# Two streams of a transformer-and-scan kernel: the next sequence's front moved into the FFN, scan units recut, mask on TensorE, one-hots and a quarter of the products on GpSimd

## The chip, the cores and the metric

The kernel runs on one core of a Trainium2 chip. The metric is the device time of one launch in microseconds (us), lower is better. It computes two post-norm decoder layers for 16 sequences of 256 tokens with 256 features.

## The reference

Each line is followed by a residual add and a layer norm (`x = layernorm(x + f(x))`):

```
layer 0  mamba:   xin, z = split(x @ W_in)            # 512 channels each
                  xc = silu(causal_conv4(xin) + conv_b)
                  dt, Bm, Cm = split(xc @ W_xproj)    # 64, 16, 16 columns
                  dt = softplus(dt @ W_dt + b_dt)
                  h_t = exp(dt_t * A) * h_{t-1} + dt_t * B_t * xc_t   # 512 x 16 states, 256 steps
                  y_t = sum_n(h_t * C_t);  out = ((y + xc * Dp) * silu(z)) @ W_out
         latent cross-attention: 16 heads of 16; each query attends to 64 keys given by
                  itok (with repeats: a count of each key acts as weight, no count as mask)
         FFN with quantised activations and ternary weights, 256 -> 1024 -> 256, gelu, layer norm inside
layer 1  self-attention (16 heads of 16), cross-attention (16 heads of 64),
         mixture of 8 experts (top 6) and a shared expert
```

## The kernel before

**Two streams.** Layer 0 of sequence i (the x stream: `mamba`, `latent`, `ffn`, `ffn_end`) runs at the same time as layer 1 of sequence i-1 (the y stream: self-attention, cross-attention, experts). Every engine has one instruction list. Each engine's part of either stream is written as a generator whose `yield`s cut it into steps, and `ORDER` says by hand for each engine in which turn steps of x and y are taken ("x9 y3 ..."). Nothing reorders it later: an instruction that waits holds up all that stands behind it on its engine. The engines meet in semaphores. PSUM (`ps`) has eight banks pairs-wise called `bank(n)`: 0 to 3 for x, 4 to 7 for y. `region_x` and `region_y` are SBUF scratch that the stages of a stream reuse.

**The mamba stage.** TensorE (PE) projects x with `win` in four parts (L497, `projected`). ScalarE (ACT) scales by the last tap (L983), VectorE (DVE) adds the other three taps (L1383, twelve operations of 128x256), ACT takes silu. PE multiplies by `wxd` (low rank, L516), `wc` and `wb` (C and B with each of the 16 rows repeated over 8 partitions, L519, L549) and `wdt` (L543), and ACT and DVE compute softplus (L1406 to L1411) and dt times xc (L1413). The rows of dt and dt·xc go to DRAM (`rows_of_dt`) and come back spread over partitions, 64 DMAs a sequence of 256 KB each (L329, `spread_rows`, four slots each).

**The scan** is cut into 32 units. A unit has 8 channels x 16 states on the partitions and two channel groups along the free axis: ACT forms the decay by two exponentials into PSUM (L1028), DVE the product dtx·B (L1432, `product`, B read from PSUM), then the scan (L1449), POOL (GpSimd) multiplies by C (L1227), and PE sums the states (L561).

**Counts and masks.** The 64 indices of each query are split in two digits (`digits`). DVE writes one-hot rows of both digits (L1351, `one_hots`), PE multiplies them query by query (L471, `counted`, four parts of 32), turns the result (L480, `counts_turned`) and turns it again by key (L489); DVE makes `cntq`, `mask` and `cntk` of it (L1361, L1362, L1368). In `narrow_attention` of the latent stage, DVE takes the row maximum of the scores under the mask with a custom operation for each half (L1482, 32 a sequence, each with a read of its accumulator and half of them with a memset); self-attention has no mask and takes one plain reduce for four (L1486).

**The FFN of x** is w1 (L694), gelu, norm, quantisation, turns (L706), w2 (L713). The one-hots and counts of the next sequence are already taken in it; the projection, convolution and all that follows come behind it.

## Time and profile before

| | us |
|---|---|
| median of 3 runs | 3937.22 (3931.72 to 3943.57) |
| the profiled execution | 3951.12, of it span 3949.3 |
| PE busy | 3210.4 (81%) |
| DVE busy | 3004.6 (76%) |
| ACT busy | 1953.3 (49%) |
| POOL busy | 650.5 (16%) |
| steady period of one sequence | 232.8 |

The span is the time from the first to the last instruction in the trace. The period was read in the middle of the run, and is cut in three stages: A from the end sum of the latent stage to the first product of the scan (FFN and front of x, experts of y), B to the last scan, C (latent attention of x, rest of cross-attention of y) to the next sum.

### The profile page before, as it was taken

The page shows a single profiled execution, that of the slowest core. Times are in us where ns is not written, and L with a number is a line of the kernel's source. Part 1 is how long each engine was busy: PE and PEld are TensorE (multiplying, and loading weights), DVE is VectorE, ACT ScalarE, POOL GpSimd, SP SyncE. Part 2 cuts the span into 40 slices and gives each one's busy share as a digit, 9 for nine tenths or more (in the row PEclk, how much of TensorE's full clock was granted, in tenths as well). Part 3 has the DMA queues.
Part 4 walks back from the last instruction along what each step waited for, and adds up shares of the span by engine and source line. Part 5 has one row for each costly group of instructions (what it writes and reads, how often), then busy time and mean ns, then how long its engine had stood idle before and what let it go on. Part 6 is the DMA issues. An engine that isn't in the chain of part 4 may idle for free.

```text
span 3949.3 us, 57618 instructions
## 1 busy us (share of the span) xinstructions
PE 3210.4 (81%) x21250; PEld 2199.1 (56%) x21250; DVE 3004.6 (76%) x6496; ACT 1953.3 (49%) x4513; POOL 650.5 (16%) x516
## 2 busy tenths in 40 slices
PE   2468988788797888978888897988879888887877
PEld 1245656556464655646556564655646565564655
DVE  5678796877878688796868879687887868778632
ACT  2336455564545546455554645555464554645422
POOL 0303030120303012040210304021030301204000
PEclk8679999999999989999999999989999998999987
DMA  6526171532716235181523517153361614427100
GB/s 213 131 56 174 50 197 63 157 119 89 203 50 184 77 123 153 54 238 49 155 95 116 171 50 225 52 159 99 96 196 50 197 63 146 130 74 215 55 31 16
DMA packets 205833, 470.84 MB, mean 119 GB/s; under 512 B 23856, under 2 KB 43952, under 8 KB 190832
## 3 DMA queue, kind: packets, MB, share of 16 engines
q1 hardware_dynamic: 205552, 467.17, 39.2%
q8 instruction: 167, 2.74, 0.3%
q14 instruction: 114, 0.93, 0.1%
HBM read 446.11 MB, written 20.97 MB: 118 GB/s over the span
## 4 chain that ended last, share of the span: by engine, by line
PE 41%; DVE 34%; ACT 9%; issue 8%; DMA 6%; SPq 1%; POOL 0%; DVEq 0%; ACTq 0%
DVE region_x L1449 7%; PE ps L864 6%; DMA region_x<-rows_of_dt 5%; DVE region_x L1432 5%; PE ps L633 4%; PE ps L824 3%; PE ps L810 3%; PE ps L497 3%; ACT region_y L1148 3%; PE ps L845 3%; PE ps L614 2%; DVE nm L1486 2%; PE ps L645 2%; DVE x_stats L1284 2%; PE ps L569 2%
## 5 line engine op out<-in xcount | busy, mean ns | idle before, releaser
L1227 POOL TENSOR_TENSOR region_x<-region_x 128x512 f32<-128x512 f32 x512 | 650.3, 1270 | 2982.6 <-DVE region_x L1449 2982.6
L1028 ACT ACTIVATE ps<-region_x,aneg 128x255 f32<-128x255 f32 x1024 | 443.1, 470 | 446.2 <-DVE region_x L1449 431.3
L1449 DVE TENSOR_TENSOR_SCAN region_x<-ps,region_x 128x512 f32<-128x512 f32 x512 | 622.9, 1217 | 16.0 <-ACT ps L1028 15.1
L1432 DVE TENSOR_TENSOR region_x<-region_x,ps 128x512 f32<-128x512 f32 x512 | 343.1, 671 | 49.2 <-DMA region_x<-rows_of_dt 46.2
L864 PE MATMUL ps<-xTy,wide 128*128 128x256 f32 x1280 | 307.1, 395 | 0.0
L1148 ACT ACTIVATE region_y<-ps,rmax 128x256 f32<-128x256 f32 x512 | 235.7, 500 | 140.9 <-DVE rmax L1591 140.9
L1499 DVE SCALAR_TENSOR_TENSOR region_x<-region_x,cntk 128x512 f32<-128x512 f32 x256 | 167.0, 689 | 156.2 <-ACT region_x L1066 156.2
L864 PEld LDWEIGHTS ps<-xTy,wide 128*128 128x128 f32 x1280 | 244.5, 196 | 42.3 <-issue 10.1
L561 PE MATMUL ps<-region_x,sely 128*32 128x512 f32 x1024 | 157.5, 691 | 121.6 <-POOL region_x L1227 121.3
L614 PE MATMUL ps<-region_y 64*128 64x256 f32 x1024 | 176.9, 485 | 91.5 <-DVE VP L1572 37.4
L633 PE MATMUL ps<-region_y 64*128 64x256 f32 x1024 | 173.1, 464 | 95.9 <-ACT region_y L1066 49.5
L1591 DVE TENSOR_REDUCE rmax<-ps 128x4 f32<-128x1024 f32 x128 | 153.2, 1218 | 111.2 <-PE ps L791 109.7
L1482 DVE CUSTOM_DVE_ANT_0 region_x<-ps,mask 128x256 f32<-128x256 f32 x512 | 184.7, 420 | 40.1 <-issue 40.1
L925 PE MATMUL ps<-down,region_y 128*128 128x256 f32 x640 | 183.4, 454 | 37.2 <-DVE region_y L1650 37.2
L1164 ACT ACTIVATE region_y<-ps 128x512 f32<-128x512 f32 x256 | 140.6, 597 | 142.1 <-PE ps L813 142.1
L633 PEld LDWEIGHTS ps<-region_y 64*128 64x128 f32 x1024 | 103.0, 217 | 190.9 <-ACT region_y L1066 131.3
L614 PEld LDWEIGHTS ps<-region_y 64*128 64x128 f32 x1024 | 113.4, 236 | 155.0 <-DVE nm L1486 60.6
L1066 ACT ACTIVATE region_x<-ps 128x512 f32<-128x512 f32 x256 | 141.2, 605 | 86.6 <-PE ps L633 86.6
L925 PEld LDWEIGHTS ps<-down,region_y 128*128 128x128 f32 x640 | 146.0, 233 | 64.9 <-issue 38.7
L791 PE MATMUL ps<-region_y 64*128 64x256 f32 x1024 | 138.7, 406 | 41.7 <-DVE region_y L1586 24.6
L1066 ACT ACTIVATE region_y<-ps 128x512 f32<-128x512 f32 x256 | 138.3, 593 | 52.9 <-PE ps L633 52.0
L810 PE MATMUL ps<-region_y 64*128 64x256 f32 x1024 | 156.5, 397 | 8.9 <-ACT shiftT L1157 7.6
(246 smaller groups left out, 6491.9 us busy)
## 6 DMA issues: line engine op xcount, KB each, us to landing
region_x<-rows_of_dt SPq DMA_DIRECT2D x1024, 256.0 KB, 5.3
wide<-in_wgate SPq DMA_DIRECT2D x16, 1280.0 KB, 8.4
wide<-in_wup SPq DMA_DIRECT2D x16, 1280.0 KB, 11.0
down<-in_wmoe SPq DMA_DIRECT2D x16, 1280.0 KB, 5.6
wide<-in_wq SPq DMA_DIRECT2D x16, 1024.0 KB, 4.8
wide<-in_wk SPq DMA_DIRECT2D x16, 1024.0 KB, 6.9
wide<-in_wv SPq DMA_DIRECT2D x16, 1024.0 KB, 8.9
down<-in_wo SPq DMA_DIRECT2D x16, 1024.0 KB, 7.8
```

Source lines behind the costliest of these rows:

```text
L614: last = mm(ps[:, b + j, qt * T:(qt + 1) * T], a.QT[r, t, qt * P:(qt + 1) * P], a.KT[u % 2][r, t, :], start=True, stop=True)
L633: last = mm(ps[:, a.sT_bank(n + j), kt * T:(kt + 1) * T], a.KT[e][r, t, kt * P:(kt + 1) * P], a.QT[r, t, :], start=True, stop=True)
L810: mm(ps[:, b, kt * T:(kt + 1) * T], KT2[r, t, kt * P:(kt + 1) * P], QT2[r, t, :], start=True, stop=False)
L864: last = mm(bank(b)[:, j, :], w[:, k, f * P:(f + 1) * P], xTy[:, k, :], start=(k == 0), stop=(k == KD - 1))
L925: last = mm(bank(7)[:, tt, :], mhT[:, f, tt * P:(tt + 1) * P], wmoe[:, f, :], start=(n == 0), stop=(n == KM - 1))
L1028: last = f(ps[:, 1 + 2 * (k % 2), m * T + 1:(m + 1) * T], dt_rep[k % SLOTS][:, m, 1:T], ACT.Exp, scale=aneg[:, k, m:m + 1])
L1066: f(a.PT[:, n % 8].rearrange("p k q -> p (k q)"), ps[:, a.sT_bank(n), :], ACT.Exp).then_inc(a.probs, 1)
L1148: last = f(junk2[:, 4 * (u % 2) + 2 * qt + g], ps[:, a.pair_bank(u) + g, qt * T:(qt + 1) * T], ACT.Exp, bias=rmax[:, qt, g, u:u + 1], accu ...
L1227: nc.gpsimd.tensor_tensor(hbuf[k % HSLOTS], hbuf[k % HSLOTS], csb.unsqueeze(1).to_broadcast([P, 2, T]), ALU.mult).then_inc(hc_ready, 1)
L1432: tt_(hbuf[k % HSLOTS], dtx_rep[k % SLOTS], ps[:, 2, 0:T].unsqueeze(1).to_broadcast([P, 2, T]), ALU.mult).then_inc(dbx, 1)
L1449: nc.vector.tensor_tensor_scan(flat(hbuf[k % HSLOTS]), ps[:, 1 + 2 * (k % 2), :], flat(hbuf[k % HSLOTS]), 0.0, ALU.mult, ALU.add).then_inc ...
L1482: last = nc.vector.tensor_tensor_reduce(a.junk[:, 4 * (u % 2) + 2 * qt + j], ps[:, b + j, qt * T:(qt + 1) * T], mask[:, qt, :], -1.0, HUGE ...
```

## The change

1. **Front inside the FFN.** `projected`, the convolution, silu, `low_rank`, dt, the first half of softplus and all one-hots of sequence i+1 are issued inside `ffn(i)`; `counted`, `c_and_b` and `counts_turned` at its end. The digits move to the latent stage. `region_x` grows, so that the buffers live beside those of the FFN.
2. **Convolution.** ACT forms all four tap products from PSUM (16 operations a sequence), POOL adds them (6 of 128x512). DVE's twelve operations go.
3. **Low rank, B and C.** One matrix `wx` of 96 columns (4 matmuls) and four matmuls with `rep`, which repeats the rows, stand for the twelve of `wxd`, `wc` and `wb`. ACT copies C and B to SBUF.
4. **Scan units.** A unit has 16 channels x 8 states on the partitions and two halves of the states along the free axis. Both halves use the same dt row, so a spread DMA brings 128 KB in place of 256 KB, and there are eight slots. The sum over states now has 64 matmuls of 256 columns in place of 32 of 512.
5. **Mask on PE.** `mask` is bf16, and two matmuls with the identity bring it into PSUM ahead of the scores (16 a sequence, 128x512). The maximum is the plain reduce (now L1573).
6. **One-hots on POOL** (L1310, 48 of 128x128), and every fourth product too (L1333). Also from DVE to ACT: the adds of `bdt` (4), the copy to `VP0`, the scaling of `QT2` (4).
7. New order tables for all engines (one row shown).

```diff
-SLOTS = 4
+SLOTS = 8
...
-    "pe": (67, "x9 y3 x1 y13 x1 y2 x1 y6 x1 y4 x1 y7 x1 y4 x1 y3 x1 y5 x1 y1 x1 y1 x2 y2 x1 y2 x5 y3 x1 y1 x1 y1 x1 "
+    "pe": (60, "y2 x1 y12 x1 y7 x1 y5 x1 y3 x1 y8 x1 y3 x1 y7 x2 y1 x1 y1 x2 y2 x1 y2 x5 y2 x2 y1 x1 y1 x1 y2 x1 y2 "
...
-                pair, s, j = k // 16, k % 16 // 4, k % 4
-                first = 32 * j + 8 * s
-                rows = scratch[i % 2, what][first:first + 8, 512 * pair:512 * pair + 512]
-                return sp.dma_start(dst.rearrange("p m t -> p (m t)"), rows.unsqueeze(0).to_broadcast([NS, 8, 512]))
+                m, e, j = k // 8, k // 4 % 2, k % 4
+                first = 32 * j + 16 * e
+                rows = scratch[i % 2, what][first:first + 16, T * m:T * m + T]
+                return sp.dma_start(dst, rows.unsqueeze(1).to_broadcast([16, 8, T]))
...
+                    if a.masked:
+                        pe.wait_ge(cnt_max, i + 1)
+                        for j in range(2):
+                            mm(ps[:, b + j, :], W["identb"][:], mask[:].rearrange("p q k -> p (q k)"), start=True, stop=False)
...
+                if more:
                     pe.wait_ge(f_h, at(i, TT, 2))
-                    yield from counted(i + 1, 0, 2)
+                    projected(i + 1, 2)
+                    projected(i + 1, 3)
+                    yield from low_rank(i + 1)
+                    pe.wait_ge(silu_z, i + 2)
+                    yield from counted(i + 1, 0, 1)
...
+            def conv_products(i, half):
+                act.wait_ge(xz, at(i, 4, half + 1))
+                act.wait_ge(digit_step, at(i, DIGIT_STEPS, DIGIT_STEPS))
+                if half:
+                    act.wait_ge(conv_sum, at(i, 6, 3))
+                for j in range(2):
+                    m = 2 * half + j
+                    f(conv[:, m, :], bank(half)[:, j, :], ACT.Identity, bias=W["convb"][:, m:m + 1],
+                      scale=W["convw"][:, m, TAPS - 1:TAPS])
+                    for k in range(TAPS - 1):
+                        late = TAPS - 1 - k
+                        last = f(taps[k][:, j, late:T], bank(half)[:, j, 0:T - late], ACT.Copy,
+                                 scale=W["convw"][:, m, k:k + 1])
+                last.then_inc(taps_sb, 1)
...
+            def one_hot(o, digit, first, last):
+                for value in range(first, last):
+                    ins = nc.gpsimd.tensor_scalar(o[:, :, value], digit, float(value), None, ALU.is_equal)
+                return ins
+
+            def next_sequence(i):
+                pool.wait_ge(digit_step, at(i, DIGIT_STEPS, DIGIT_STEPS))
+                if i:
+                    pool.wait_ge(X.sum_ps, at(i - 1, 3, 2))
+                one_hot(oh_lo, lob, 0, 16)
+                conv_sums(i, 0)
+                one_hot(oh_hi, hib, 0, 8)
+                conv_sums(i, 1)
+                one_hot(oh_hi, hib, 8, 32).then_inc(onehot, 1)
...
+                for k in range(UNITS):
+                    if k % 4 == 2 and k + 5 < UNITS:
+                        product(k + 5)
                     pool.wait_ge(h_ready, at(i, UNITS, k + 1))
...
-                    if a.masked:
-                        if u >= 2:
-                            v.wait_ge(a.rmax, at(i, 8, u - 1))
-                        for qt in range(TT):
-                            nc.vector.memset(spare[:, 6 + 2 * (u % 2) + qt:7 + 2 * (u % 2) + qt], 0.0)
-                            for j in range(2):
-                                col = 64 * j + 32 * (u % 2) + 16 + t
-                                last = nc.vector.tensor_tensor_reduce(
-                                    a.junk[:, 4 * (u % 2) + 2 * qt + j], ps[:, b + j, qt * T:(qt + 1) * T], mask[:, qt, :],
-                                    -1.0, HUGE, ALU.add, ALU.min, a.NM[:, qt, col:col + 1])
```

**TensorE, from the last counts of the FFN to the turn of the counts, before.** L471 are the counts (`counted`), L925 the experts' down projection of y, L706 and L713 the turns and w2 of the FFN, L497 the projection, L516 to L549 low rank, C, dt and B, L480 the counts turned.

```order
L471 MATMUL ps<-region_x 32x16 x32
L925 MATMUL ps<-down,region_y 128x256 x10
L706 MATMUL ps<-identb,region_x 128x128 x16
L713 MATMUL ps<-w2q,region_x 128x256 x16
L471 MATMUL ps<-region_x 32x16 x32
L497 MATMUL ps<-xTx,win 128x256 x4
L471 MATMUL ps<-region_x 32x16 x32
L497 MATMUL ps<-xTx,win 128x256 x12
L516 MATMUL ps<-region_x,wxd 64x256 x2
L519 MATMUL ps<-region_x,wc 128x256 x2
...
L543 MATMUL ps<-region_x,wdt 128x256 x4
...
L480 MATMUL ps<-identb,region_x 128x32 x16
```

The same stretch of TensorE after, in two pieces: first from the cross-attention's output (L864, L845 before) on, then the end. L502 is the projection, L883 the experts (L864 before), L889 the routing weights, L511 `wx`, L518 `wdt`, L478 the counts, L529 and L534 `rep`, L487 the counts turned.

```order
L864 MATMUL ps<-down,region_y 128x256 x16
L502 MATMUL ps<-xTx,win 128x256 x8
L466 MATMUL ps<-ident,xh 128x128 x4
L873 MATMUL ps<-router,xTy 128x8 x4
L883 MATMUL ps<-xTy,wide 128x256 x8
L687 MATMUL ps<-identb,region_x 128x128 x2
...
L883 MATMUL ps<-xTy,wide 128x256 x4
L502 MATMUL ps<-xTx,win 128x256 x8
L883 MATMUL ps<-xTy,wide 128x256 x4
L889 MATMUL ps<-wT,selx 128x256 x2
L883 MATMUL ps<-xTy,wide 128x256 x8
L511 MATMUL ps<-region_x,wx 96x256 x4
```

```order
L518 MATMUL ps<-region_x,wdt 128x256 x2
L478 MATMUL ps<-region_x 32x16 x32
L717 MATMUL ps<-identb,region_x 128x128 x8
L944 MATMUL ps<-down,region_y 128x256 x10
...
L478 MATMUL ps<-region_x 32x16 x32
L730 MATMUL ps<-w2q,region_x 128x256 x16
L529 MATMUL ps<-region_x,rep 128x256 x2
L534 MATMUL ps<-region_x,rep 128x256 x2
L944 MATMUL ps<-down,region_y 128x256 x10
L478 MATMUL ps<-region_x 32x16 x64
L487 MATMUL ps<-identb,region_x 128x32 x16
```

The projections and low rank have moved from behind w2 to between the experts' matmuls, and only the B and C rows, half of the counts and their turn still stand behind w2. All 16 matmuls of the cross-attention's output (L864) stand behind the latent output now; before, they stood ahead of it in two halves, with the latent stage's turns between them (L662, L668).

**VectorE, from the end of the FFN to the first scan, before.** L1395 adds `bdt`, L1361 to L1362 are `cntq` and `mask`, L1406 to L1413 softplus and dt·xc, once for each half.

```order
L1395 TENSOR_SCALAR region_x<-ps,bdt 128x256 x2
L1361 COPY cntq<-ps 128x256
L1362 TENSOR_SCALAR mask<-ps 128x256
L1361 COPY cntq<-ps 128x256
L1362 TENSOR_SCALAR mask<-ps 128x256
L1406 TENSOR_SCALAR region_x<-region_x 128x512
...
L1368 COPY cntk<-ps 128x512
L1406 TENSOR_SCALAR region_x<-region_x 128x512
...
L1416 MEMSET ps 128x2 x2
L1432 TENSOR_TENSOR region_x<-region_x,ps 128x512 x2
```

VectorE there after; L1495 is dt·xc of the second half, L1475, L1476 and L1482 are `cntq`, `mask` and `cntk`, L1529 the product and L1549 the scan.

```order
L1495 TENSOR_TENSOR region_x<-region_x 128x512
L1505 MEMSET ps 128x2
L1475 COPY cntq<-ps 128x256
L1476 TENSOR_SCALAR mask<-ps 128x256
L1475 COPY cntq<-ps 128x256
L1476 TENSOR_SCALAR mask<-ps 128x256
L1482 COPY cntk<-ps 128x512
L1511 MEMSET ps 128x2
L1529 TENSOR_TENSOR region_x<-region_x,ps 128x512 x2
L1549 SCALAR_TENSOR_TENSOR region_x<-ps,region_x 128x512
```

Softplus and dt·xc of both halves now stand ahead of the masks instead of behind them.

**GpSimd after**, from the last units of one sequence on (before, its whole list is the multiplications by C): L1341 are these, L1310 the one-hots, L1306 the sums of the convolution, L1333 the products.

```order
L1341 TENSOR_TENSOR region_x<-region_x 128x512 x6
L1310 TENSOR_SCALAR region_x<-region_x 128x128 x16
L1306 TENSOR_TENSOR region_x<-region_x 128x512 x3
L1310 TENSOR_SCALAR region_x<-region_x 128x128 x8
L1306 TENSOR_TENSOR region_x<-region_x 128x512 x3
L1310 TENSOR_SCALAR region_x<-region_x 128x128 x24
L1333 TENSOR_TENSOR region_x<-region_x 128x512
L1341 TENSOR_TENSOR region_x<-region_x 128x512 x2
```

Ahead of TensorE's first count (L478) all 48 one-hots have to be done.

## Rows read from the trace of the kernel before

**Rows 1.** The page: busy time, and the chain that ended last, by engine.

```profile
PE 3210.4 (81%) x21250; PEld 2199.1 (56%) x21250; DVE 3004.6 (76%) x6496; ACT 1953.3 (49%) x4513; POOL 650.5 (16%) x516
...
PE 41%; DVE 34%; ACT 9%; issue 8%; DMA 6%; SPq 1%; POOL 0%; DVEq 0%; ACTq 0%
```

**Rows 2.** Windows: us, busy PE, PEld, DVE, ACT, POOL; clock, DMA share, GB/s.

```profile
1606.60:1684.60 78.00, 67.65 (x442) 52.94 (x442) 67.64 (x166) 36.64 (x63) 0.00 (x0) 0.96 0.21 76
1684.60:1765.00 80.40, 60.91 (x366) 35.67 (x368) 76.15 (x102) 42.15 (x97) 39.44 (x32) 0.92 0.83 231
1765.00:1839.40 74.40, 68.06 (x524) 46.85 (x520) 42.65 (x140) 43.07 (x123) 1.23 (x1) 1.00 0.15 58
sum 232.80, PE 196.62 PEld 135.47 DVE 186.45 ACT 121.85 POOL 40.67; mean PE 65.54 PEld 45.16 DVE 62.15 ACT 40.62 POOL 13.56
```

**Rows 3.** The chain in stage A, its last part: start, us, link.

```profile
1653.17 1.05 PE ps L713 x8
...
1669.39 1.92 PE ps L549 x8
1671.32 1.11 PE ps L480 x16
...
1688.67 1.13 DVE region_x L1449
```

**Rows 4.** TensorE's timeline near the end of stage C (two records a matmul).

```profile
1828.22 3.72 PE L845 MATMUL ps<-down,region_y 128*128 128x256 f32 x16
...
1832.65 3.62 PE L845 MATMUL ps<-down,region_y 128*128 128x256 f32 x16
```

**Rows 5.** Groups by line and form: busy us, mean ns, idle before them.

```profile
L1227 POOL TENSOR_TENSOR region_x<-region_x 128x512 f32<-128x512 f32 x512 | 650.3, 1270 | 2982.6 <-DVE region_x L1449 2982.6
L1432 DVE TENSOR_TENSOR region_x<-region_x,ps 128x512 f32<-128x512 f32 x512 | 343.1, 671 | 49.2 <-DMA region_x<-rows_of_dt 46.2 <-DMA rows_of_dt<-region_x 1.0
L1482 DVE CUSTOM_DVE_ANT_0 region_x<-ps,mask 128x256 f32<-128x256 f32 x512 | 184.7, 420 | 40.1 <-issue 40.1
L1482 DVE DVE_READ_ACCUMULATOR2_ANT nm<- 128x1 f32 x512 | 42.7, 83 | 0.0
L1486 DVE TENSOR_REDUCE nm<-ps 128x4 f32<-128x1024 f32 x128 | 153.0, 1216 | 12.8 <-PE ps L614 9.4
L1383 DVE SCALAR_TENSOR_TENSOR region_x<-region_x,convw 128x256 f32<-128x256 f32 x192 | 84.6, 482 | 22.2 <-ACT region_x L983 19.3
L1351 DVE TENSOR_TENSOR region_x<-region_x,iota 128x1024 bf16<-128x1024 bf16 x64 | 77.6, 1212 | 0.1
L1351 DVE TENSOR_TENSOR region_x<-region_x,iota 128x512 bf16<-128x512 bf16 x64 | 43.8, 685 | 0.0
L1586 DVE TENSOR_SCALAR region_y<-ps 128x512 f32<-128x512 f32 x64 | 42.3, 681 | 15.9 <-PE ps L779 15.9
L983 ACT ACTIVATE region_x<-ps,convb,convw 128x256 f32<-128x256 f32 x64 | 32.4, 562 | 0.0
L694 PE MATMUL ps<-w1q,region_x 128*128 128x512 bf16 x128 | 31.9, 395 | 0.7 <-ACT region_x L1084 0.7
```

**Rows 6.** VectorE's timeline in stage B.

```profile
1706.59 1.22 DVE L1449 TENSOR_TENSOR_SCAN region_x<-ps,region_x 128x512 f32<-128x512 f32 x1
1707.72 0.66 DVE L1432 TENSOR_TENSOR region_x<-region_x,ps 128x512 f32<-128x512 f32 x1
1708.31 1.22 DVE L1449 TENSOR_TENSOR_SCAN region_x<-ps,region_x 128x512 f32<-128x512 f32 x1
...
1720.15 0.69 DVE L1432 TENSOR_TENSOR region_x<-region_x,ps 128x512 f32<-128x512 f32 x1 [1.15 <-DMA region_x<-rows_of_dt]
```

**Rows 7.** Timeline at 1743.7, and line L1297's instructions (ns lowest, median, highest).

```profile
1743.69 1.26 POOL L1227 TENSOR_TENSOR region_x<-region_x 128x512 f32<-128x512 f32 x1 [0.44 <-DVE region_x L1449]
1743.70 1.28 DVE L1297 SCALAR_TENSOR_TENSOR y_nt<-y_nt,y_rstd 128x2 f32<-128x2 f32 x1
...
L1297 DVE SCALAR_TENSOR_TENSOR y_nt<-y_nt,y_rstd x48: 160/161/1280, 342.0 to 3945.6; 128x2 f32<-128x2 f32 x48
```

## Prediction before the change was run

> **What bounds the kernel now.** I read the page first [rows 1]. TensorE is busy for 81% of the span and VectorE for 76%, and the chain that ended last is split between them, 41% and 34%; neither alone is the bound, so I cut one steady period in the three stages named above and read the windows [rows 2]. In A TensorE works 67.65 of 78.0 us and VectorE 67.64. In B VectorE works 76.15 of 80.4 us and TensorE 60.9. In C TensorE works 68.1 of 74.4 and VectorE 42.7. So VectorE sets B, TensorE sets C, and A has both near 87%. For A I read the chain [rows 3]: TensorE is on it without a break from w2 at 1653.2 to the end of the turned counts at 1672.4, then come masks, softplus and the DMA round trip of the dt rows, and the first scan starts at 1688.7. From TensorE's last turn to the first scan pass 16.2 us, in which TensorE has other work but VectorE has no scan.
>
> The profiled execution took 3951.12 us, 1.82 more than its span; the median of the runs is 0.9965 of it. All sums below are made against the span.
>
> **VectorE's removals, per sequence.** From the groups [rows 5], each divided by 16 sequences. The taps: 84.6 / 16 = 5.3 us. The one-hots: (77.6 + 43.8) / 16 = 7.6. The masked maximum: (184.7 + 42.7) / 16 = 14.2 and 16 memsets, under 1 us together, replaced by eight plain reduces of 1.216 as self-attention has, 9.7: 5 saved. Eight products: 8 x 0.67 = 5.4. Four `QT2` scalings: 42.3 / 16 = 2.6, the `VP0` copy at the same price 0.7, and four adds of `bdt` of half that width, 0.4 each, 1.7. In all 28 of 186.5 us, so VectorE needs about 158.
>
> **TensorE.** It gains 16 bf16 matmuls of 512 columns with the mask. The group of w1, the same form, has 31.9 / 128 = 0.25 us each: +4.0. Four matmuls fewer in the projection of B, C and low rank, at 1.92 / 4 = 0.48 [rows 3]: -2. The sum over states keeps its columns; its extra 32 issues lie in B, where TensorE has 19 us idle, and cost nothing there (at 0.1 us each they would be 3). So TensorE goes from 196.6 to about 199, and it becomes the engine that all hangs on: below 199 no period can go, and 232.8 - 199 is what packing could give at most.
>
> **ACT and POOL.** ACT takes 12 more tap products at 0.5 (the group of the last tap has 0.56 on average [rows 5]), the `bdt` adds, copies and `QT2`, and gives up some: 121.9 to about 133. POOL goes from 40.7 to: 38 + 8 of 1.27 more for products, 6 x 1.27 = 7.6 for sums, and 48 one-hots. A one-hot of one input and 128 columns is not in the trace. POOL's two-input operation costs 1.27 / 512 = 2.5 ns a column, so 128 columns are 0.32, and with something fixed I take 0.39. Bounds: 0.15 (VectorE's per-column price, 1.212 / 1024, on 128 columns), and 1.27 for a whole one of the widest form seen. At 0.39 it is 18.7 us a sequence, and POOL has 78 us of 233.
>
> *The skill on this.* The Trainium skill, "GPSIMD Engine Reference", § Engine selection, has two-input elementwise work about twice as slow on GpSimd as on VectorE and one-input work at about line rate; the product row agrees (1.27 against 0.67), and by line rate a one-hot would be nearer my lower bound than the upper.
>
> **Stage A after.** TensorE's list in A: before, 65.8 us lay between the latent sum and the end of L480 (1672.4 - 1606.6). Now the 16 matmuls of the cross-attention's output (3.7 + 3.6 = 7.3 [rows 4]) lie behind the latent output, and 2 go: 71.1 if every idle stays. The windows show 10.3 us of TensorE idle in A; without any it would be 61. I followed the new list by hand against ACT (tap products to 13.6 us after the sum, second half 17.5 to 21.5, since `conv_products` waits for POOL's first sums; w1's start at 24.6, against 23.4 before) and against POOL (last one-hot at 34.7, first count due at 46.7, so 12 us of slack), and get the turned counts' end at 67.0. Behind it VectorE no longer waits for softplus and the dt rows: these are done during the FFN, and the spread DMAs are under way. There remain the turn by key (behind eight query projections, 3.9 us), one copy, a memset and the product: first product at 72.5 at the earliest. I add 1.5 for hand-overs that the walk leaves out, and 3 for the shared lock.
>
> The lock is in the trace: a VectorE operation of 128x2 whose median is 0.16 us takes 1.28 beside a POOL operation of 1.26, and ends with it [rows 7]. POOL was idle in A [rows 2]; now it works some 26 us there (18.7 + 7.6), while VectorE has about 40 operations with two SBUF inputs. One in three meets POOL (26 of 78), and loses half of 0.39 or of 1.27: near 3 us. From below it is 0, if VectorE waits for others anyway; from above half of POOL's time, 13. So A comes to 77, against 78.0.
>
> **Stage B after.** VectorE's work 76.2, less eight products at the spacing with which they stand between scans (1708.31 - 1707.72 = 0.59 [rows 6]), 4.7, less `QT2`'s 2.4, plus the self-attention's scaling that now falls in it (1.9): 71. The idle was 4.3 us, of which 46.2 / 16 = 2.9 waiting for the spread DMAs, as in the row at 1720.15. The DMA share in B is 0.83. Halving the bytes at the same count of packets gives something between no relief (a packet costs its turn) and half; with eight slots I take 2.5 of idle. B = 73.5. POOL does not bind: per unit it needs 1.27 x 1.25 = 1.59, VectorE 1.13 + 0.75 x 0.59 = 1.57 of scan and product (1707.72 - 1706.59 = 1.13) plus its y work.
>
> **Stage C after.** TensorE sets it: 74.4 - 7.3 (moved to A) + 4.0 (mask) - 0.6 (its waits for the masked maximum) = 70.5.
>
> **Sum.** 77 + 73.5 + 70.5 = 221.0 against 232.8: 11.8 a period, 15 periods, 177. The first sequence has no FFN to hide in: its one-hots cost 18.7 on POOL in place of 7.6, the sums 2.3 more and the taps wait for them, some +15, less 7 for the shorter way to the first scan: +8. Span 3949.3 - 177 + 8 = 3780; with 1.82 and 0.9965: **3769 us**.
>
> **Rivals.**
> *R1, slower: the one-hots hold up TensorE.* The first count waits for all 48, and behind it stand turns, w2 and the experts' down projection. By the walk the slack is 12 us over 48 operations: it decides at 0.39 + 12 / 48 = 0.64 that a stall begins, and it eats the gain of 11.8 at 0.9. At 1.27 the stall is 48 x 1.27 - 30.7 = 30: period 251, span near 4270. At 1.1 the period is 243 and the time 4130 (15 x 22 us, and as much once in the first sequence). For it speaks that POOL's fixed cost is nowhere to be read beside a strided write, against it that the two-input operation itself is 2.5 ns a column. 0.06, at some 4130.
> *R2: A does not get denser.* The lock, the wait of the second tap products for POOL, and ACT's longer list push w1 and all behind it: 6 us more, A = 83, period 227, 3860. For it: 40 operations against a busy POOL, and ACT's 0.5 us steps stand before qT and gelu. 0.15. The Trainium skill, "SBUF — State Buffer", § Who interferes with whom, says that a VectorE operation with two SBUF inputs and a GpSimd one that reads SBUF block each other wholly; the row at 1743.7 agrees (1.28 for 0.16), and the page speaks against handing POOL work in A.
> *R3: the new order packs TensorE.* If its share in B also rises as VectorE's 28 us fall away, and A and C lose idle, 199 / 0.94 = 212, span 3641, 3634. For it: VectorE falls to 158 and nobody else is above 133. Against: each of TensorE's idles in A is a dependence inside a stream. 0.14.
> *R4: no change*, the FFN's stage growing by all that the scan's saves: 0.03.
>
> **Chances.** The forecast has 0.62, own range 3720 to 3815 (the lock 0 or 6, the DMA idle 0 or 3, hand-overs, times 15). The range for all, 3660 to 3865, takes in R2 and the slower half of R3. About 0.3% is what a measurement can tell here. Faster: 0.62 + 0.15 + 0.14 = 0.91; same 0.03; slower 0.06.
>
> **What would show it.** The period near 221, TensorE's busy share near 0.9 from 0.81; L1310 near 0.39 us, ended before the first L478 wants it; first product 73 to 80 us behind the latent sum; no DMA behind the first scan; VectorE at 158 a period; L1529's wait for spread DMAs under 1 us a sequence. Wrong would be: TensorE waiting for POOL's L1310 or for ACT's tap products at w1, or two-input VectorE operations in A near 1.3 us.

## The result, and the profile after

The changed kernel takes 4131.91 us (median, 4130.08 to 4133.3) against 3940.39 of the kernel before in the same series: 1.0484 of its time, 95% interval 1.0462 to 1.0506. The forecast was 3769. The time that came is that of the rival R1, which had 0.06.

The page of the changed kernel: busy time, the chain that ended last by engine, and by line.

```profile
PE 3258.6 (79%) x22402; PEld 2261.6 (55%) x22402; DVE 2714.0 (66%) x4787; ACT 2040.2 (49%) x4788; POOL 1744.8 (42%) x1508
...
PE 40%; POOL 20%; DVE 13%; ACT 12%; issue 6%; DVEq 0%; ACTq 0%; POOLq 0%
POOL region_x L1310 18%; PE ps L608 6%; DVE region_x L1549 5%; PE ps L944 4%; PE ps L627 4%; PE ps L749 4%; ACT ps L1066 3%; PE ps L843 3%; PE ps L829 3%; DVE region_x L1529 3%; POOL region_x L1306 3%; PE ps L810 2%; PE ps L639 2%; ACT region_y L1215 2%; PE ps L604 2%
```

VectorE's busy time has fallen from 3004.6 to 2714.0 us, which is 18 us a sequence where 28 were forecast, and the waits for spread DMAs are gone from the chain [rows 1]. But GpSimd, which had 0% of it, now holds a fifth of it, nearly all with the one-hots (L1310). The three stages of one period:

```profile
1697.20:1792.07 94.87, 72.27 (x446) 57.19 (x445) 59.08 (x140) 38.24 (x71) 59.66 (x54) 0.86 0.21 76
1792.07:1866.80 74.73, 60.26 (x422) 39.35 (x422) 69.95 (x91) 45.99 (x106) 48.59 (x39) 0.98 0.38 118
1866.80:1939.50 72.70, 67.71 (x539) 43.23 (x536) 39.85 (x69) 42.66 (x122) 1.46 (x2) 1.00 0.15 61
sum 242.30, PE 200.25 PEld 139.77 DVE 168.89 ACT 126.89 POOL 109.70; mean PE 66.75 PEld 46.59 DVE 56.30 ACT 42.30 POOL 36.57
```

Against [rows 2], B fell from 80.4 to 74.7 (forecast 73.5) and C from 74.4 to 72.7 (forecast 70.5), but A rose from 78.0 to 94.9 (forecast 77), with GpSimd busy for 59.7 us of it. The line of the one-hots, its own view: duration lowest, median and highest in ns, and who waited for it. Then its group, with the mean.

```profile
L1310 POOL TENSOR_SCALAR region_x<-region_x x768: 954/983/2011, 40.8 to 3697.6; 128x128 bf16<-128x128 bf16 x192
...
  PE ps L478: 273.6, 16
```

```profile
L1310 POOL TENSOR_SCALAR region_x<-region_x 128x128 bf16<-128x128 bf16 x768 | 821.9, 1118 | 1150.1 <-PE ps L669 1069.3
```

No one-hot took under 0.95 us, and the mean is 1.12, where the forecast had 0.39. TensorE waited for the last of them in each of the 16 sequences. Its timeline in this period:

```profile
1745.35 1.13 PE L518 MATMUL ps<-region_x,wdt 64*128 64x256 f32 x4
1760.10 1.00 PE L478 MATMUL ps<-region_x 128*32 128x16 bf16 x32 [13.62 <-POOL region_x L1310]
...
1761.86 6.68 PE L944 MATMUL ps<-down,region_y 128*128 128x256 f32 x20
...
1773.59 4.58 PE L944 MATMUL ps<-down,region_y 128*128 128x256 f32 x20
...
1785.10 6.16 PE L749 MATMUL ps<-xTy,wq 128*128 128x256 f32 x16 [0.69 <-ACT xTy L996]
```

The first count stands idle for 13.6 us. Behind it, ten matmuls of the experts take 6.7 us, and ten of the same form 4.6 a little later; eight query projections take 6.2, and the eight key projections of the same form 3.6 to 3.7 in the runs below. These stretches, and the engine's idle one before them, have a granted clock below 1, that is, part of them at 1.2 GHz and not at 2.4:

```profile
1746.50:1760.00 13.50, 0.00 (x0) 0.00 (x0) 6.91 (x10) 0.00 (x0) 12.83 (x11) 0.60 0.35 105
1760.00:1770.00 10.00, 9.90 (x102) 8.53 (x103) 0.00 (x0) 5.30 (x8) 0.00 (x0) 0.69 0.84 330
1770.00:1780.00 10.00, 9.23 (x83) 7.49 (x82) 3.56 (x13) 2.30 (x5) 0.00 (x0) 1.00 0.01 4
1780.00:1792.00 12.00, 9.93 (x75) 8.11 (x72) 7.16 (x21) 2.83 (x8) 0.00 (x0) 0.72 0.28 89
```

The first sequence has nothing to hide its one-hots in: TensorE waits 60.5 us there.

```profile
PE ps L478 <- POOL region_x L1310: 60.5, 1, 60.5
```

### The profile page after: what moved, and what is told of

It is laid out like the page before. It is cut to its first block, busy times and chain, and to the rows that moved or that the text cites. A ratio compares the mean times of both kernels' runs of the same rounds, so it can differ in the third digit from the quotient of the medians.

```text
span 4131.5 us, 59728 instructions
## 1 busy us (share of the span) xinstructions
PE 3258.6 (79%) x22402; PEld 2261.6 (55%) x22402; DVE 2714.0 (66%) x4787; ACT 2040.2 (49%) x4788; POOL 1744.8 (42%) x1508
## 4 chain that ended last, share of the span: by engine, by line
PE 40%; POOL 20%; DVE 13%; ACT 12%; issue 6%; DVEq 0%; ACTq 0%; POOLq 0%
POOL region_x L1310 18%; PE ps L608 6%; DVE region_x L1549 5%; PE ps L944 4%; PE ps L627 4%; PE ps L749 4%; ACT ps L1066 3%; PE ps L843 3%; PE ps L829 3%; DVE region_x L1529 3%; POOL region_x L1306 3%; PE ps L810 2%; PE ps L639 2%; ACT region_y L1215 2%; PE ps L604 2%
## 5 line engine op out<-in xcount | busy, mean ns | idle before, releaser
L1310 POOL TENSOR_SCALAR region_x<-region_x 128x128 bf16<-128x128 bf16 x768 | 821.9, 1118 | 1150.1 <-PE ps L669 1069.3
L1341 POOL TENSOR_TENSOR region_x<-region_x 128x512 f32<-128x512 f32 x512 | 644.8, 1273 | 378.6 <-DVE region_x L1549 375.8
L1549 DVE TENSOR_TENSOR_SCAN region_x<-ps,region_x 128x512 f32<-128x512 f32 x512 | 614.8, 1214 | 8.3 <-ACT ps L1066 6.6
L1573 DVE TENSOR_REDUCE nm<-ps 128x4 f32<-128x1024 f32 x256 | 308.9, 1222 | 147.3 <-PE ps L608 142.2
L1333 POOL TENSOR_TENSOR region_x<-region_x 128x512 f32<-128x512 f32 x128 | 162.8, 1272 | 526.2 <-DVE region_x L1529 494.1
L883 PE MATMUL ps<-xTy,wide 128*128 128x256 f32 x1280 | 334.5, 414 | 0.4 <-DVE region_y L1724 0.4
L478 PE MATMUL ps<-region_x 128*32 128x16 bf16 x2048 | 62.5, 171 | 288.6 <-POOL region_x L1310 273.6
L883 PEld LDWEIGHTS ps<-xTy,wide 128*128 128x128 f32 x1280 | 255.4, 206 | 51.7 <-issue 9.9
L1215 ACT ACTIVATE region_y<-ps,rmax 128x256 f32<-128x256 f32 x512 | 235.7, 498 | 74.4 <-DVE rmax L1665 74.4
L1529 DVE TENSOR_TENSOR region_x<-region_x,ps 128x512 f32<-128x512 f32 x384 | 254.9, 667 | 8.5 <-PE ps L552 8.5
L608 PE MATMUL ps<-region_y 64*128 64x256 f32 x1024 | 160.2, 455 | 80.4 <-DVE nm L1573 37.1
L478 PEld LDWEIGHTS ps<-region_x 128*32 128x32 bf16 x2048 | 57.3, 97 | 302.5 <-issue 240.1
L1000 ACT ACTIVATE region_x<-ps 32x512 bf16<-32x512 f32 x64 | 37.3, 583 | 346.6 <-PE ps L478 346.6
L627 PE MATMUL ps<-region_y 64*128 64x256 f32 x1024 | 149.0, 411 | 63.1 <-ACT region_y L1107 57.1
L1431 DVE TENSOR_TENSOR xh<-ps,xh 128x512 f32<-128x512 f32 x80 | 54.8, 685 | 199.3 <-PE ps L944 73.0
```

What stands on the lines that cost most here:

```text
L608: last = mm(ps[:, b + j, qt * T:(qt + 1) * T], a.QT[r, t, qt * P:(qt + 1) * P], a.KT[u % 2][r, t, :], start=not a.masked, stop=not a.maske ...
L627: last = mm(ps[:, a.sT_bank(n + j), kt * T:(kt + 1) * T], a.KT[e][r, t, kt * P:(kt + 1) * P], a.QT[r, t, :], start=True, stop=True)
L883: last = mm(bank(b)[:, j, :], w[:, k, f * P:(f + 1) * P], xTy[:, k, :], start=(k == 0), stop=(k == KD - 1))
L1215: last = f(junk2[:, 4 * (u % 2) + 2 * qt + g], ps[:, a.pair_bank(u) + g, qt * T:(qt + 1) * T], ACT.Exp, bias=rmax[:, qt, g, u:u + 1], accu ...
L1310: ins = nc.gpsimd.tensor_scalar(o[:, :, value], digit, float(value), None, ALU.is_equal)
L1341: nc.gpsimd.tensor_tensor(hbuf[k % HSLOTS], hbuf[k % HSLOTS], csb, ALU.mult).then_inc(hc_ready, 1)
```

## The experiments

Two theories were set against each other. Theory 1: the price of the one-hots is the whole error. Theory 2: A is slower for other reasons too (the lock, that is, VectorE and GpSimd holding each other up; ACT's list; the clock). A, B, C and the period below are read as in the table of stages, at the same place of each run, in us. One period is not the whole run: in the kernel before A goes from 78.0 to 82.6 and B from 79.3 to 82.6, and in others A varies by 1 to 4 us. So the last column has the mean of 13 periods, from the second latent sum of the run to the fifteenth.

| kernel | time | A | B | C | period | mean period |
|---|---|---|---|---|---|---|
| before | 3940.4 | 78.0 | 80.4 | 74.4 | 232.8 | 233.5 |
| the change | 4131.9 | 94.9 | 74.7 | 72.7 | 242.3 | 242.4 |
| oh_few | 3912.2 | 81.4 | 74.9 | 72.7 | 228.9 | 228.7 |
| oh_major | 3940.1 | 82.5 | 74.6 | 72.7 | 229.8 | 230.9 |
| keys_first | 4009.2 | 82.5 | 79.9 | 72.7 | 235.0 | 235.5 |
| mask_dve | 3930.5 | 84.3 | 74.7 | 72.3 | 231.3 | 230.3 |
| oh_dve | 3922.7 | 85.9 | 73.4 | 72.7 | 232.1 | 232.1 |
| oh_split | 3927.5 | 85.8 | 74.7 | 72.7 | 233.2 | 232.0 |
| sums_dve | 3917.2 | 85.4 | 73.4 | 72.7 | 231.6 | 232.0 |
| prod_dve | 3968.7 | 86.7 | 77.5 | 72.1 | 236.3 | 235.6 |
| w1_first | 3922.8 | 85.9 | 73.4 | 72.7 | 232.1 | 232.1 |
| counts_early | 3946.3 | 88.2 | 74.6 | 72.7 | 235.5 | 234.3 |
| sums_mask_dve | 3909.2 | 88.0 | 73.6 | 70.6 | 232.2 | 232.1 |
| oh_spread | 3873.0 | 82.4 | 73.4 | 72.7 | 228.5 | 228.9 |
| best | 3840.5 | 81.9 | 73.7 | 72.3 | 227.9 | 227.1 |

The times come from several series, and the kernel before was timed in each: 3952.5 beside oh_few, oh_dve and oh_split, 3943.2 beside oh_major, keys_first, mask_dve and sums_dve, 3944.5 beside prod_dve, w1_first, counts_early and sums_mask_dve, 3946.7 beside oh_spread and best. So a difference of under some 10 us between kernels of different series is not shown by their times.

**probe_pool: what a small GpSimd operation costs.** The kernel before, with single operations ahead of GpSimd's work, as

```diff
+            for k in range(4):
+                pool.wait_ge(probed, n)
+                g.tensor_scalar(pro[:, :, k], prb[:, 0:128], float(k), None, ALU.is_equal).then_inc(probed, 1)
+                n += 1
```

> The kernel before with 31 single operations put ahead of GpSimd's work, where it is idle, each waiting for the one before; the rest is unchanged. Theory A (a fixed cost): a one-hot of 128 columns took at least 0.97 us in the changed kernel since a float GpSimd operation costs about 0.9 us whatever its width; then 16 columns take 0.85 to 0.95 and 512 columns of one input about 1.3. Theory B (price per column for bf16 or for the comparison): 16 columns take under 0.3, 512 columns about 3.8, and an f32 multiply of 128 columns is clearly cheaper (0.35 to 0.5). Theory C (the stride of the output): a contiguous output takes under 0.5 where the strided one takes 0.97. Two inputs of 128 columns in f32: 0.35 to 0.45 if its price is 2.5 ns a column as at 512.

One line for each form: lowest, median, highest in ns. `pro[:, :, k]` (L1234, L1242) writes every 16th bf16 element, the rest write side by side.

```profile
L1234 POOL TENSOR_SCALAR pro<-prf x4: 954/954/966, 1.1 to 4.2; 128x128 bf16<-128x128 bf16 x4
L1238 POOL TENSOR_SCALAR pro<-prf x4: 526/526/527, 5.3 to 7.1; 128x128 bf16<-128x128 bf16 x4
L1242 POOL TENSOR_SCALAR pro<-prf x4: 300/301/301, 7.7 to 8.9; 128x16 bf16<-128x16 bf16 x4
L1250 POOL TENSOR_SCALAR pro<-prf x3: 1486/1487/1487, 11.7 to 14.8; 128x512 bf16<-128x512 bf16 x3
L1262 POOL TENSOR_SCALAR pro<-prf x3: 527/527/537, 21.2 to 22.5; 128x128 f32<-128x128 f32 x3
L1266 POOL TENSOR_TENSOR pro<-prf x3: 455/455/456, 23.1 to 24.1; 128x128 f32<-128x128 f32 x3
```

None of the three theories is right alone, and C is nearest. From 128 to 512 columns side by side (1487 - 526) / 384 = 2.5 ns a column are left, as in the two-input row [rows 5], and some 0.21 us that every operation pays. The stride adds 0.43 us at 128 columns; of the two strided rows (954 - 300) / 112 = 5.8 ns a column, with the same 0.21 us. The type and the operation make no difference (L1238 against L1262), so theories A and B fall; for C the operation without the stride is just over its 0.5. Even without the stride a one-hot would have been 0.53, not 0.39.

**oh_few: the one-hots left out.** From the second sequence on two fills stand for the 48 one-hots.

```diff
+                if i:
+                    nc.gpsimd.memset(oh_lo, 1.0)
+                    conv_sums(i, 0)
+                    conv_sums(i, 1)
+                    nc.gpsimd.memset(oh_hi, 1.0).then_inc(onehot, 1)
+                    return
```

> The changed kernel, but from the second sequence on the 48 one-hots are left out and two fills of the buffers with ones stand for them, so that the counts are not those of the indices. Theory 1 (the price of the one-hots is the whole error): TensorE's 13.6 us wait before the first count goes and with it the low clock after it (3 to 4 us), 15 times; the period falls from 242 to 221 to 225, the time to 3790 to 3870 (the first sequence keeps its wait of 60). Theory 2 (stage A would be as slow for other reasons: the lock, the tap products that wait for GpSimd, ACT's list): A stays above 86 us and the time above 3940.

The wait goes and the period falls by 13.4 us, but to 228.9 and not to 221, and the time of 3912 lies above theory 1's range and below theory 2's: each has a part. A is 81.4 with no one-hot left in it. Its windows (A, then two stretches of it), then VectorE's timeline in the first part of A, and TensorE's.

```profile
1599.50:1680.85 81.35, 71.83 (x446) 55.77 (x446) 58.27 (x140) 38.41 (x71) 13.01 (x8) 0.90 0.25 91
...
1612.80:1619.10 6.30, 6.28 (x24) 5.03 (x24) 4.84 (x14) 3.51 (x10) 2.94 (x3) 0.73 0.00 0
...
1672.00:1680.80 8.80, 8.11 (x27) 6.31 (x26) 5.56 (x15) 1.47 (x3) 0.00 (x0) 0.59 0.48 155
```

```profile
1614.80 1.11 DVE L1423 SCALAR_TENSOR_TENSOR x_rstd<-x_nt,x_rstd 128x2 f32<-128x2 f32 x1
...
1618.71 0.29 DVE L1455 TENSOR_SCALAR region_x<-region_x 128x256 f32<-128x256 f32 x1
...
1619.63 1.25 DVE L1455 TENSOR_SCALAR region_x<-region_x 128x256 f32<-128x256 f32 x1
1620.91 1.30 DVE L1456 TENSOR_SCALAR region_x<-region_x 128x256 bf16<-128x256 f32 x1
...
1625.38 1.50 DVE L1713 CAST wsplit<-route 128x16 bf16<-128x16 f32 x1
```

```profile
1612.82 1.06 PE L873 MATMUL ps<-router,xTy 128*128 128x8 f32 x8 [1.98 <-ACT xTy L996]
1613.73 5.39 PE L883 MATMUL ps<-xTy,wide 128*128 128x256 f32 x16
...
1627.65 0.27 PE L906 MATMUL ps<-identb,wsplit 128*32 128x128 bf16 x2 [3.32 <-DVE wsplit L1716]
1627.86 3.45 PE L698 MATMUL ps<-w1q,region_x 128*128 128x512 bf16 x8
...
1673.51 6.54 PE L749 MATMUL ps<-xTy,wq 128*128 128x256 f32 x16 [0.69 <-ACT xTy L996]
```

Here is what the walk through TensorE's list (the prediction's "Stage A after") had missed. The routing weights (`wsplit`) of y come late, since the FFN's norm and quantisation of x stand ahead of them on VectorE, with three operations held up by GpSimd's sums (1.11, 1.25 and 1.30 us; the second and third take 0.29 for the first half of the tokens just before). w1 stands behind them on TensorE and starts 28.4 us behind the latent sum, not 24.6. Not all of the wait of 3.32 us is the change's: the cast of 1.50 us stands beside this run's own second fill on GpSimd (3.51 us) and ends with it; the next cast of this form takes 0.17. And behind TensorE's waits for the router (1.98) and for the query projections (0.69 and, just before, 0.69) the same matmuls are slower, at a granted clock of 0.73 and 0.59 in the windows above: 5.39 us for eight of L883 against 3.7 later in this stage, 6.54 for the query projections against 3.6.

**oh_dve, oh_split: the one-hots elsewhere.** All on VectorE in 8 operations, two pairs ahead of w1's results and two behind them; or those of the low digit on GpSimd.

```diff
-                one_hot(oh_lo, lob, 0, 16)
                 conv_sums(i, 0)
-                one_hot(oh_hi, hib, 0, 8)
                 conv_sums(i, 1)
-                one_hot(oh_hi, hib, 8, 32).then_inc(onehot, 1)
...
+                if i + 1 < B:
+                    one_hots(0)
+                    one_hots(1)
                 v.wait_ge(rows_loaded, at(i, 48, 48))
```

> The changed kernel with the one-hots on VectorE again (8 operations, 7.6 us a sequence, inside the FFN), the sums of the convolution left on GpSimd. Theory 1: the wait of TensorE goes here too, and the first sequence's too; VectorE's 7.6 us in A cost 0 to 5 of them: period 222 to 229, time 3760 to 3870. Theory 2: no better than 3940.

> The changed kernel with the 16 one-hots of the low digit on GpSimd (17 us) and those of the high digit in four operations of 1.2 us on VectorE; nine low ones come ahead of the first sums. Theory 1: GpSimd is done some 26 us behind the latent sum and nothing waits for it; with 2.7 us less on VectorE than with all one-hots there, the time is the same or up to 40 us lower than in the run with all on VectorE. If the lock matters (theory 2 in part), it is higher than that run, by 16 small operations that VectorE's two-input operations wait for.

oh_dve misses the ranges of both theories: 3922.7, with 3927.5 for oh_split; they are 0.9935 (0.9918 to 0.9952) and 0.9946 (0.9929 to 0.9962) of the kernel before. A is 85.9. Moving 2.7 us of work from VectorE to 16 small GpSimd operations gains nothing; the time is 4.8 us higher, as the lock's side of the expectation had it.

**oh_major: the same 48 operations, without the stride.**

```diff
-        oh_hi, oh_lo = in_x(4352, (P, 32), BF16), in_x(10508, (P, 16), BF16)
+        oh_hi, oh_lo = in_x(4352, (32, P), BF16), in_x(10508, (16, P), BF16)
...
-                    ins = nc.gpsimd.tensor_scalar(o[:, :, value], digit, float(value), None, ALU.is_equal)
+                    ins = nc.gpsimd.tensor_scalar(o[:, value], digit, float(value), None, ALU.is_equal)
```

> The changed kernel with the one-hot buffers laid out value by value, so that each of GpSimd's 48 operations writes 128 bf16 side by side; TensorE reads them with a stride instead. The probe had 0.59 us for such a write against 1.02 with the stride. If the write's stride was the price: one-hots 28 us a sequence, done some 40 us behind the latent sum, ahead of the first count; TensorE's wait of 13.6 us goes, the period is 229 to 232 as in the run without one-hots (228.9), the first sequence waits 20 us less than there: 3890 to 3930. Rival: TensorE's strided reads make the counts dearer (32 of them took 0.97 us) and give it back.

One index order takes 192 us off the change (3940.1 against 4131.9) and brings it to the time of the kernel before (0.9997, 0.9983 to 1.001), 10 us above the expected range. Its mean period is 2.6 us shorter than that of the kernel before; what that gives is spent outside the periods, see the last part of "What it cost" below. The one-hots in this run:

```profile
L1310 POOL TENSOR_SCALAR region_x<-region_x x768: 516/527/1617, 40.8 to 3493.8; 128x128 bf16<-128x128 bf16 x192
```

The rival holds in part as well. TensorE's strided reads make each of the 128 count matmuls dearer, first in this run, then in the change:

```profile
L478 PEld LDWEIGHTS ps<-region_x x2048: 130/150/152, 76.4 to 3524.9; 128*32 128x32 bf16 x187
L478 PE MATMUL ps<-region_x x2048: 199/207/230, 76.4 to 3524.9; 128*32 128x16 bf16 x187
```

```profile
L478 PEld LDWEIGHTS ps<-region_x x2048: 92/94/114, 95.8 to 3719.3; 128*32 128x32 bf16 x187
L478 PE MATMUL ps<-region_x x2048: 169/170/196, 95.8 to 3719.3; 128*32 128x16 bf16 x187
```

32 of them take 1.99 us in place of 0.97, 4 us a sequence.

**keys_first: TensorE's order, one entry.** On oh_major:

```diff
-    "pe": (60, "y2 x1 y12 x1 ...
+    "pe": (60, "y1 x1 y13 x1 ...
```

> The run before this one (one-hots value by value) with one entry of TensorE's order changed: the turn of the counts by key comes ahead of self-attention's eight query projections, which took 6.5 us at a clock of about 0.5 where the forecast had 3.9. If these projections at the low clock hold up the first product: it starts 2 to 4 us sooner, and the time is 30 to 60 us lower. Rival: VectorE in B is filled by self-attention, which now starts later, and the total stays within 12 us.

Wrong by its sign, and more than the rival: 69 us slower. A stays at 82.5 in this period. TensorE now idles for the mask ahead of the turn by key, and all of self-attention starts later; B grows from 74.6 to 79.9.

```profile
PE ps L496 <- DVE mask L1476: 4.6, 1, 4.6
```

The projections at the low clock were cover for a wait, not its cause.

**mask_dve and sums_mask_dve: the mask on VectorE again**, on oh_major and on sums_dve; `tensor_tensor_reduce` for each half as in the kernel before.

```diff
-                    if a.masked:
-                        pe.wait_ge(cnt_max, i + 1)
-                        for j in range(2):
-                            mm(ps[:, b + j, :], W["identb"][:], mask[:].rearrange("p q k -> p (q k)"), start=True, stop=False)
```

> One-hots value by value, and the mask taken on VectorE again as in the kernel before (32 custom operations of 0.42 us with accumulator reads, an f32 mask, no matmuls for it). The mask's 16 matmuls take 4.8 us a sequence. If TensorE alone sets stage C, the time falls by 40 to 70 us; rival: the custom operations stand in the chain of the scores (about 2.2 us for a pair of heads instead of 1.2), and the time rises by up to 60 or stays.

> The run with one-hots and sums on VectorE (3917.2), and the mask's maximum there too, no matmuls for the mask. With the one-hots value by value this step gave 10 us; if it is TensorE's 4.8 us less in C against custom operations of 5 us more on VectorE, it gives the same here: 3895 to 3915. Rival: VectorE, now at its load of the kernel before but for products and taps, is longer in C, and the time rises.

mask_dve is 9.6 us under oh_major: the right sign, and far from 40 to 70. sums_mask_dve is 8.0 under sums_dve, within its expected range, but the two are of different series (0.9913, 0.9895 to 0.993, against 0.9935, 0.991 to 0.9961) and their mean periods are the same, so this gain is not shown. On the mean of the 13 periods C falls by 1.3 and 1.8 us only, though TensorE does 3 us less in it, and A rises by 1.1 and 1.8. So the mask on TensorE neither cost nor gave much.

**sums_dve: nothing on GpSimd in A**, on oh_dve; the six additions move to VectorE.

```diff
-                    nc.gpsimd.tensor_tensor(part, part, taps[k], ALU.add).then_inc(conv_sum, 1)
+                    tt_(part, part, taps[k], ALU.add).then_inc(conv_sum, 1)
...
+                if i + 1 < B:
+                    conv_sums(i + 1, 0)
                 yield from quantised(i, c, hn, D, 2)
                 if i + 1 < B:
+                    conv_sums(i + 1, 1)
```

> The run with the one-hots on VectorE, and the six sums of the convolution there too, 4.1 us a sequence; GpSimd does nothing in the FFN. Against that run (3922.7): if the lock between the two engines costs as much in A as single operations show (1.11 us for 0.16, 1.25 for 0.29), VectorE wins back 3 to 5 us a sequence and the time is 0 to 40 us lower; if the lock is nothing, VectorE's 4.1 us more make it 30 to 60 higher.

3917.2 against 3922.7, in different series; each is 0.9935 of the kernel before beside it, and the mean period is 232.0 against 232.1. So the time did not change, although VectorE took over six operations of 0.69 us, 4.1 in all. Stage A of oh_dve, then of this run:

```profile
1576.72:1662.65 85.93, 72.04 (x447) 55.61 (x446) 64.16 (x148) 38.40 (x71) 8.81 (x6) 0.90 0.23 83
```

```profile
1575.88:1661.32 85.44, 70.90 (x445) 55.22 (x446) 63.78 (x154) 38.16 (x71) 0.00 (x0) 0.90 0.23 82
```

VectorE has six operations more and is busy for 0.4 us less. So its other operations took some 4.5 us less: that much it had lost beside 8.8 us of GpSimd work.

**prod_dve: all products on VectorE**, on oh_dve.

```diff
-                    if k % 4 == 3:
-                        return
                     v.wait_ge(rep_dtx[k % SLOTS], at(i, 64, 16 * (k // SLOTS + 1)))
```

> The run with the one-hots on VectorE, with all 32 products on VectorE. The forecast priced the eight on GpSimd at 4.7 us a sequence in stage B: then this run is 60 to 75 us slower. Rival: B is held by the chain of self-attention's scores on TensorE (moving its start by 3 us moved B by 5 in the run with the keys first), and VectorE's 4.7 us go into waits it has anyway: 0 to 25 us slower.

46 us slower, between the two expected ranges; B grows by 4.0 us (3.8 on the mean), where the forecast had 4.7. This term of the sum holds nearly.

**w1_first and counts_early: two exchanges in TensorE's list**, on oh_dve: w1 ahead of the routing transposition, for which TensorE waits 5.8 us there (two turns of the order), and the third and fourth part of the counts ahead of w2 (ACT's copies to match).

```diff
-    "pe": (60, ... x2 y3 x1 y1 x1 y2 x2 y2 x1 y3 ...
+    "pe": (60, ... x2 y3 x1 y1 x1 y1 x2 y3 x1 y3 ...
```

```diff
-                    yield from counted(i + 1, 1, 2)
+                    yield from counted(i + 1, 1, 4)
...
                     yield from c_and_b(i + 1)
-                    yield from counted(i + 1, 2, 4)
```

> The run with the one-hots on VectorE (3922.7), with two entries of TensorE's order exchanged: the first FFN product w1 comes ahead of the transposition of the routing weights (the experts' of y), for which TensorE waits 5.8 us there (3.3 us in the run without one-hots), and after which w1 runs 3.6 us in place of 1.9. If this wait and the clock behind it are what stage A has beyond the forecast: A falls by 3 to 6 us, the time to 3835 to 3880. Rival: w1 was not what is late (the experts' chain is), the wait appears at the next step of y, and the time stays within 12 us.

> The run with the one-hots on VectorE, with the third and fourth part of the counts ahead of w2 instead of behind the experts' down projection, so that the thin matmuls of 16 columns no longer stand right ahead of self-attention's projections (6.5 us where at full clock they take 3.6). Clock theory: the projections run in 4 us or less, the first product is 2 to 3 us earlier, 30 to 45 us in all. Rival: the hand-overs of the counts to ACT (0.77 us each) now stall TensorE ahead of w2, or VectorE is not ready earlier, and the time is the same or up to 30 us higher.

w1_first: w1 takes 1.89 us instead of 3.59 and starts 24.7 us behind the latent sum instead of 31.0, and the period is the same to a tenth. TensorE in this run:

```profile
1602.58 1.89 PE L697 MATMUL ps<-w1q,region_x 128*128 128x512 bf16 x8
1608.54 0.37 PE L905 MATMUL ps<-identb,wsplit 128*32 128x128 bf16 x2 [4.08 <-DVE wsplit L1711]
...
1609.91 3.78 PE L882 MATMUL ps<-xTy,wide 128*128 128x256 f32 x8
...
1634.33 6.20 PE L943 MATMUL ps<-down,region_y 128*128 128x256 f32 x20
```

A wait of 4.1 us stays, and the four matmuls behind it take 3.78 us where oh_dve has 2.37. When L943 starts, this kernel is still 1.8 us ahead of oh_dve, counted from the latent sum; its ten matmuls take 6.20 us instead of 4.54, at a granted clock of 0.72, and that takes back the 1.8. counts_early is 24 us slower, its rival: TensorE waits 2.4 us for y's norm instead of 0.7 and w2 takes 3.01 us instead of 1.92.

**oh_spread and best.** On oh_dve the four pairs of one-hots are put apart; best has that, the sums and the mask on VectorE.

```diff
                 if i + 1 < B:
                     one_hots(0)
-                    one_hots(1)
...
-                    one_hots(2)
-                    one_hots(3)
+                    one_hots(1)
...
                     yield from dt_half(next_steps, i + 1, 0)
+                    one_hots(2)
+                    one_hots(3)
```

> The run with the one-hots on VectorE (3922.7), with the four pairs apart: the first ahead of the FFN's w1 as there, the second behind it, the third and fourth behind the FFN's second quantisation and the first half of softplus, where VectorE waits for TensorE. In that run two pairs (3.8 us) stand on VectorE ahead of the routing weights, for which TensorE waits 5.8 us, and two ahead of the FFN's norm. If VectorE's queue in the first 50 us of A is what is left: A falls from 85.9 to 82 to 84, the time to 3865 to 3900. Rival: the clock takes it back, as when w1 was put first (the freed time came back as slower matmuls), and the time stays within 12 us.

> All that helped together: one-hots on VectorE spread as in the run beside it, the convolution's sums and the mask's maximum on VectorE too; GpSimd keeps the multiplications by C and a quarter of the products. If the gains add up (5 for the sums, 8 for the mask, and what the spreading gives): 3855 to 3895, 1.2 to 2.2% below the kernel before. Rival: VectorE is then at 175 us a sequence and its own bound in A: 3900 to 3920.

oh_spread: 3873.0, 50 us under oh_dve for the same work, A 82.4. The mean period is 3.2 us shorter, which is 47 us in 15 periods. TensorE's wait for `wsplit` is 4.1 us instead of 5.8. best: 3840.5 us, 0.974 (0.9713 to 0.9767) of the kernel before; it beats both ranges. Its sum row:

```profile
sum 227.88, PE 196.66 PEld 138.35 DVE 175.36 ACT 126.73 POOL 50.11; mean PE 65.55 PEld 46.12 DVE 58.45 ACT 42.24 POOL 16.70
```

The single steps (50, and 5.5 and 8 that are not shown apart) add to 63; together they gave 82. VectorE has 6.5 us more to do than in the change, and the kernel is 291 us faster, 209 of them by the first step, oh_dve: at 175 of 228 us VectorE is still not the bound.

## Why the prediction was wrong, by its steps

**The step that failed: the price of a one-hot.** "At 0.39" should have been 1.12 (0.95 at least). It came from the per-column price of a wide operation whose output lay side by side; the write to every 16th or 32nd element was not priced at all, though R1 names "a strided write". The two-input row gave the columns rightly (2.5 ns), the probe puts 0.21 us of fixed cost and 0.43 for the stride on top; the rest up to 1.12 are operations prolonged beside VectorE's (up to 2.01): in the first sequence, where VectorE has little to do, the mean is 0.97, and each of the 193 that are over 0.1 us longer than the median overlaps a VectorE operation with its inputs in SBUF. The 0.06 of R1 was the second part of the fault: the bounds reached to 1.27 and the case was decided at 0.64, so more than half of the range lay on the wrong side. R1's numbers came out (at 1.1 a period of 243 and 4130, measured were 242.3 and 4132), but its working only in part, so that the closeness is luck as well. At 1.12 it has a stall of 48 x 1.12 - 30.7 = 23 us; the trace has 13.6, since the last one-hot ends 62.8 us behind the latent sum and not 69.7, and the first count was due at 49.3 and not at 46.7. The rest of the 21.3 us comes from terms that R1 did not have.

**What it cost.** The period is 21.3 us above the forecast's. 13.4 of it are shown by oh_few to be the one-hots, the slower matmuls behind the wait included; A has 4.4 more without them, B 1.2 and C 2.2. Over the whole run, cut at the end of the first and of the last latent sum (the middle column is the first with the forecast's 8 and 177 us applied):

| us | before | forecast | the change |
|---|---|---|---|
| to the first latent sum | 213.0 | 221.0 | 252.2 |
| 15 periods | 3494.4 | 3317.4 | 3626.1 |
| behind the last latent sum | 241.9 | 241.9 | 253.3 |

The periods are 309 us dearer than forecast, the first sequence 31 (TensorE waits 60.5 there), and the end 11, which the forecast did not have at all: 351, the distance from 3780 to the span of 4131.5. The end is 9 to 12 us longer in each kernel with the new order (250.7 to 254.2); what makes it so is not known. The one-hots are not the whole error either: oh_few, which takes 220 us off, is still 143 above 3769. And oh_major, with a mean period of 230.9 against 233.5, is no faster than the kernel before, because it reaches the first latent sum at 232.0 and needs 250.7 behind the last.

**Stage A.** 77 with the low price; oh_few has 81.4. Right: the slack within 3 us (first count due at 49.3 for 46.7). Missed: the routing weights behind the FFN's norm on VectorE, 3.3 us of wait in oh_few (up to 1.3 of it by that run's own fill), and the clock after waits, which the walk took as in [rows 2]. The lock was put at 3 us and sums_dve makes it some 4.5 for the additions alone.

**Stage B.** 74.7 for 73.5. The products were worth 4.0 (4.7 forecast), and VectorE's waits for DMAs in [rows 6] are gone: none is left at the product, where the forecast took 2.5 us of idle. The range's end "no relief" is excluded. But VectorE still idles 4.8 us of B (74.7 less 69.95 busy), because it now waits for TensorE's scores of self-attention, a wait that the forecast put at nothing and that the kernel before does not have in this stage:

```profile
DVE nm L1573 <- PE ps L608: 3.4, 3, 2.1
```

**Stage C.** 72.7 for 70.5. The mask's 16 matmuls took 4.8 and not 4.0, TensorE's busy time is 67.7 where the forecast implied 64.8; beside the mask the sum over states in pieces of 256 columns takes 0.8 us more in C, and the scores of the two streams 0.7 and 0.6. mask_dve shows that this stage gives back little when they go.

**VectorE's total** fell to 168.9, not 158. The operations that went are not the reason. Added up one by one, VectorE's operations in the period take 207.2 us before and 181.3 after: 31 us of them went, and those that lie on both sides are together 5.2 longer, mostly short ones in A beside GpSimd. The busy time counts overlapping stretches once (0.66 for a spacing of 0.59 [rows 6]), and the overlap shrank from 20.7 to 12.4 us; the forecast took durations, mostly single ones, off a busy time.

**R2** had the right ingredients at about the size of what oh_few left (A 81.4 for 83, period 228.9 for 227). **R3** did not come in any run: w1_first brought w1 6.3 us forward in TensorE's list and nothing came of it.

The Trainium skill has one-input elementwise work at about line rate on GpSimd ("GPSIMD Engine Reference", § Engine selection). The probe disagrees: 1.49 us for 128x512 of one input, more than the 1.27 of GpSimd's own two-input operation and than VectorE's 0.68 for as many columns from PSUM [rows 5], and 0.53 against 0.46 for one input and two at 128 columns. Its rule on blocking ("SBUF — State Buffer", § Who interferes with whom) agrees with the trace, and for its other case too, `tensor_scalar` and casts from SBUF in a mode that uses both ports: the operations of 1.25, 1.30 and 1.50 us above have one tensor as input, in SBUF. Which mode they ran in no trace shows.

What stays open: how A's last 4 us over the forecast divide between the routing weights, the lock and the clock; no run changed the clock by itself. oh_spread shows that VectorE's queue ahead of TensorE is a lever (50 us with TensorE's list unchanged), and w1_first that this one gain inside TensorE's list alone is not. A list in which the routing comes ahead of the quantisation on VectorE, with ACT's and TensorE's orders to match, was not tried.

## What to carry to other kernels

Before work goes to an engine that is idle, measure one operation of exactly that form, its stride too, and divide the slack by their number: here 12 us over 48 operations left 0.25 us each, and a stride took 0.43. When an unmeasured price decides the sign, its chance comes from where the threshold lies between the bounds, not from the hope in the middle. And where several engines are each at 70 to 85%, where the work stands in the queues is worth more than how much there is: spreading four pairs of one-hots gave 50 us, and best has 1.5 us more VectorE work a period than oh_dve and is 82 us faster. Two more things the forecast left out belong in the sum: what stands before the first and behind the last period, and the wait that comes up when the old one is gone, as VectorE's for TensorE in B.

## What the runs showed of the hardware that was not expected

- A GpSimd operation of one input: 0.53 us for 128 columns and 1.49 for 512 when it writes side by side; 0.30 for 16 and 0.95 for 128 columns written 32 bytes apart. At 128 columns, bf16 with a comparison and f32 with a multiplication: no difference.
- VectorE lost some 4.5 us a sequence beside 8.8 us of GpSimd additions (oh_dve against sums_dve), and GpSimd's one-hots lost too: 1.12 us on average for 0.95.
- TensorE reads operands with a stride of 256 bytes more slowly: weight load 0.15 us instead of 0.09, matmul of 16 columns 0.21 instead of 0.17.
- Time won inside TensorE's list can come back whole as slower matmuls at a lower granted clock (L943: 6.20 us for 4.54 at 0.72): 232.1 us a period before and after w1_first.
